# Causal keys cut in 128-blocks of one axis, and the order of the first stacks and shifts, in a four-layer attention kernel

## The chip, the cores and the metric

The kernel runs on one core of one Trainium2 chip. The metric is the device time of one launch in microseconds (us). TensorE is written PE in the rows, VectorE DVE, ScalarE ACT, GpSimd POOL, SyncE SP; SPq and ACTq are the queues on which SP and ACT issue DMAs.

## The reference

Four layers are applied to x (4 batches of 1024 tokens, 256 wide, 16 heads of 16). The change touches the first two; the third (attention with a given mask and weights) and the fourth (attention with folded weights) keep their code.

```
def _L0_xattn_ref(x, context, ...):
    qkv = (_ln(x, g1, be1) @ w_qkv + b_qkv).reshape(b, t, 3, h, dh)
    ckv = (context @ w_ckv + b_ckv).reshape(b, s, 2, h, dh)      # s = 77
    k = concatenate([k_self, k_ctx]); v = concatenate([v_self, v_ctx])
    scores = einsum('bthd,bshd->bhts', q, k) * scale
    mask = (j >= t) | (j <= i)           # own keys causal, context always seen
    x = x + softmax(where(mask, scores, -inf)) @ v
    x = x + gelu(_ln(_ln(x, g2, be2), gf, bf) @ w1 + b1) @ w2 + b2
def _L1_xattn_ref(x, encoder_out, ...):  # linear attention over the context and
    ...                                  # a causal window of 64 own keys, then Wout
    return residual + combined @ Wout
```

## The kernel before

The first three parts ("causal", the feed-forward "ff", and "window") are one program over one list of tokens, made by `front_order` (line 227). Every engine walks the same list and does its own part of each token, so the order of a token holds for all engines, SP's DMA issues included.

**The causal layer.** For each batch b, tokens are normalised (`stats`, `norm`, `flip`), projected to q and k (`qk`, `kc`), and cut into three bf16 terms (`high`, `middle`) that SP writes to DRAM (`zk`, `zq`). For each quad q of four heads SP reads them back as a stack (`stack`: 12 DMAs with the six products of terms on 96 rows, and for b = 0 one more, the row of ones from `zone`): `qs[q]` for the queries, `ks[q]` for the keys. Keys stand on one axis: 77 of the context first, then the 1024 own keys.

For a quad, the maximum of each query's scores is found first: `ring` tokens (56 a quad, lines 746 and 748 on TensorE, the maximum by VectorE at line 1016) pass through three PSUM banks (0, 1, 7). Then the `shift` token transposes the 32 x 128 maxima (L752), VectorE copies them to `nmT` (L1029), and ACT issues the DMA that puts them in row 96 of `qs[q]` (L847). The quad's first `scores` wait for that DMA (`shift_loaded`). The ring tokens of the next quad are spread over the first part of the main tokens of this quad by `spread`; the shift stands eight tokens before the quad's end, and no ring token stands behind it until the next quad starts.

The main work of a quad has two halves c of 512 queries, each made of steps (`causal_steps`, line 88). A step is one block of keys against n columns of queries: `scores` (L773: keys as the weights, four heads, two PSUM banks a shot, one or two shots), exp by ACT (L902), a diagonal mask by POOL where needed (L679), and `values` (L797: four heads side by side in the array, fp32), two steps later. Block 0 is the context (77 keys); the others are own keys by 128. So c = 0 has n = 512, 512, 384, 256, 128 and c = 1 has n = 512, 512, 384, 256, 128, 512, 512, 512, 512: 5632 columns and 24 shots a quad, over 16 quads. `vals` (L736) makes the values of each block; for the context it is two fp32 matmuls of 256 columns.

**Order around the change.** In the causal layer the list has stack 0 and stack 1 of batch 0, then `rest` (the loads of x of batches 1 to 3, L584), then the writes of the second half of the projections and the stacks 2 and 3; the ring of quad 0 follows. In the window layer, stack 0 of batch 0 waits for the last but one group of `down` products, and stack 1, 2 and 3 and the load of `wout` for the last `down`, since they lie in the memory of `hT`; `begin_rest` also has POOL's memset of v1 and VectorE's of the PSUM bank.

Of the kernel before, what the change touches and what calls it, by code (L numbers as in the profile page):

```python
# [33 lines left out]
P = 128  # L34
B, T, D, H, S = 4, 1024, 256, 16, 77
NT, ND = T // P, D // P
DH = D // H
# [49 lines left out]

def causal_steps(c):
# [66 lines left out]
def attention_tokens(ring_jobs, steps_of, nch, first):  # L155
# [76 lines left out]
def front_order():  # L232
# [18 lines left out]
    timed += [(0.6, (2, "begin")), (6.45, (2, "load_wc")), (7.99, stacks[0]), (10.0, (2, "begin_rest"))]  # L251
    timed += [(10.1, t) for t in stacks[1:]]
# [228 lines left out]
def attention_layer(nc, a, sem, x, ident, identb, masks, ctxT, banks, first, tiles_, zone, order, ring, before):  # L481
# [4 lines left out]
    steps_of = causal_steps if first else window_steps  # L486
    nch = 2 if first else 4
# [10 lines left out]
    if first:  # L498
        be, bcol, bcc, vrow, vcrow = (tiles_[n] for n in ("be", "bcol", "bcc", "vrow", "vcrow"))
# [4 lines left out]
    loaded, wc_loaded, wout_loaded, x_first, x_rest, wf_loaded, ones_saved = map(  # L504
        sem, ("loaded", "wc_loaded", "wout_loaded", "x_first", "x_rest", "wf_loaded", "ones_saved"))
    filled, const_ready, ones_ready, v_ready, cleared = map(sem, ("filled", "const_ready", "ones_ready", "v_ready", "cleared"))
    folded, tiled = sem("folded"), sem("tiled")
    nload = 8 + B if first else 3
# [37 lines left out]
    def sync(sp):  # L546
# [8 lines left out]
        def step(token):  # L555
            what, *args = token
            if what == "begin" and first:
# [6 lines left out]
                load_row(sp, vcrow, a["L0_xattn_b_ckv"][D:2 * D], loaded)  # L564
# [14 lines left out]
            elif what == "begin_rest":  # L579
                sp.wait_ge(*before["used"])  # L580
                load_weight(sp, wout, a["L1_xattn_Wout"], wout_loaded)
            elif what == "rest":
                for b in range(1, B):
                    sp.dma_start(x[:, b], a["x"][b].rearrange("(i p) d -> p i d", p=P)).then_inc(x_rest, 16)  # L584
# [5 lines left out]
            elif what == "stack":  # L590
# [27 lines left out]
    def gpsimd(pool):  # L618
# [28 lines left out]
        def step(token):  # L647
# [3 lines left out]
            if what == ("begin" if first else "begin_rest"):  # L651
# [4 lines left out]
                pool.memset(v1[:, :, :, DH:DH + 1], 1.0).then_inc(v_ready, 1)  # L656
            if what == "middle" or what == "high" and args[0]:
# [31 lines left out]
    def tensor(pe):  # L689
        started = set()  # L690
        def step(token):
# [38 lines left out]
            elif what == "vals":  # L730
                b, i = args
                rows = S if i < 0 else P
                for k in range(ND):
                    tokens_, wv = (ctxT[:, b, k, :], wc[:, k, D:2 * D]) if i < 0 else \
                        (xnT[:, k, i * P:(i + 1) * P], w[:, k, 2 * D:3 * D])
                    ins = pe.matmul(bk[0:rows, 0:D], tokens_, wv, start=k == 0, stop=k == ND - 1)  # L736
# [16 lines left out]
            elif what == "scores":  # L753
# [14 lines left out]
                for p_, pair in enumerate(pairs):  # L768
                    for side in range(2):
                        for blk, col, query, n in pieces:  # L770
                            key, nk = (0, S) if blk == 0 else (S + P * (blk - 1), P)
# [6 lines left out]
            elif what == "values":  # L778
# [15 lines left out]
                for blk, col, query, n, begins in one.gives:  # L794
                    rows = S if blk == 0 else P
# [30 lines left out]
    def scalar(act):  # L826
        def step(token):
# [57 lines left out]
            elif what == "scores":  # L885
# [7 lines left out]
                rows = S if pieces[0][0] == 0 else P  # L893
# [26 lines left out]
    def vector(dve):  # L920
        chain = Chain(dve, sem("chain"))
        def step(token):
# [23 lines left out]
            if token[0] == "stats" and token[1] == 1 and token[2] == 0 and first:  # L946
                dve.wait_ge(x_rest, 16 * (B - 1))
# [32 lines left out]
            elif what == "vals":  # L980
# [4 lines left out]
                rows = S if i < 0 else P  # L985
                dst = v1[0:rows, 1 + i, :, 0:DH]
                src = bk[0:rows, 0:D].rearrange("p (h d) -> p h d", d=DH)
                if first:
                    row = (vcrow if i < 0 else vrow)[0:rows, :].rearrange("p (h d) -> p h d", d=DH)
# [255 lines left out]
def front_layers(nc, a, sem, start, x, ident, identb, masks, ctxT, banks, masked):  # L1245
# [31 lines left out]
    def stacks(t, tag, put):  # L1277
        t["qs"], t["ks"] = [], []
        for q in range(NQ):
            t["qs"].append(put(f"qs{q}_{tag}", [KR + 1, QH, T], BF16))  # L1280
            t["ks"].append(put(f"ks{q}_{tag}", [KR + 1, QH, KW], BF16))
# [4 lines left out]
    stacks(causal, "causal", front)  # L1286
# [3 lines left out]
    for n, shape in (("wc", [P, ND, 2 * D]), ("xh", [P, NT // 2, D]), ("vrow", [P, D]), ("vcrow", [P, D]),  # L1290
                     ("be", [P, ND]), ("bcol", [P, 4]), ("bcc", [P, ND])):
# [17 lines left out]
    stacks(window, "window", Region(nc, start, LOW))  # L1309
# [3 lines left out]
    window["wc"] = top("wc_window", [P, ND, 2 * D])  # L1313
    window.update(common("window", top, middle, False))
# [3 lines left out]
    for n, shape in (("wout", [P, 4, D]), ("mixedT", [P, 2, 4, P])):  # L1318
        window[n] = top(f"{n}_window", shape)
# [11 lines left out]
              "half_used": (own_banks.ready, own_banks.filled(("down", 2 * B - 2, NT // 2 - 1))),  # L1331
# [939 lines left out]
```

## Time and profile before

| | us |
|---|---|
| runs | 2319.93, 2323.09, 2323.42 (median 2323.09) |
| the profiled execution | 2319.19 |
| its span | 2317.4 |
| mean granted clock of TensorE | 0.956 of full |

TensorE is busy 89% of the span, VectorE 61%, ACT 49%, POOL 31%. The causal layer lies at 0 to about 812 us, the feed-forward up to about 1049 us, the window layer from there to about 1600 us, and the two last layers behind it. In views of the timeline a row gives the start, the duration, the engine, the line, the operation and, in brackets, the idle time before it with what ended it; the end of a matmul is modelled and overlaps the next one, so its cost in a stream is read from the difference of two starts. An fp32 matmul leaves two records.

### The profile page before, as it was taken

Reading aid. Unit: us, or ns where it says so; the run is one execution under the profiler, and the core shown is the slowest. Engines: PE = TensorE matmul, PEld = TensorE weight load, DVE = VectorE, ACT = ScalarE, POOL = GpSimd, SP = SyncE. Lnnn points to the kernel's source line nnn. Section 1 sums busy time; section 2 is a strip of 40 time slices with the busy share of each in tenths; the row PEclk is TensorE's granted clock in tenths of the full one; section 3 lists DMA queues with packets and bytes.
Section 4 is the critical chain, followed back from the end, with each engine's and each line's share of the span. In section 5 each row is a group of like instructions: output and inputs, shape, how many; then the busy total and the mean of one; then the engine's idle time right before and its main releaser. Section 6 shows DMA issues by size and latency. Waiting matters only on the chain. (4 is left out here: it accounts for less than half of the span.)

```text
span 2317.4 us, 38184 instructions
## 1 busy us (share of the span) xinstructions
PE 2062.0 (89%) x14594; PEld 1348.2 (58%) x14594; DVE 1410.1 (61%) x3047; ACT 1132.6 (49%) x1675; POOL 729.1 (31%) x817
## 2 busy tenths in 40 slices
PE   4899999999998879996889898898989996999989
PEld 2333333343343268874466465665677775888989
DVE  4776686686768456644545455352577884766654
ACT  1265565555555666631444534444454554545444
POOL 2013113113212243411533616243301101555656
PEclk8799999999999999997999999999999998999999
DMA  5805402510630000018260613620422210000000
GB/s 122 154 6 91 76 1 60 90 23 32 111 73 1 1 14 1 10 56 125 57 115 9 135 29 67 105 65 18 141 96 83 83 56 1 8 13 12 15 12 20
DMA packets 77772, 126.65 MB, mean 55 GB/s; under 512 B 16652, under 2 KB 34828, under 8 KB 77584
## 3 DMA queue, kind: packets, MB, share of 16 engines
q1 hardware_dynamic: 74968, 122.63, 25.1%
q8 instruction: 118, 1.93, 0.4%
q10 hardware_dynamic: 2624, 1.58, 0.2%
q14 instruction: 62, 0.51, 0.1%
HBM read 93.59 MB, written 30.32 MB: 53 GB/s over the span
## 5 line engine op out<-in xcount | busy, mean ns | idle before, releaser
L1016 DVE TENSOR_REDUCE nmx_causal<-banks 128x1 f32<-128x333 f32 (+4 forms) x896 | 436.3, 537 | 174.0 <-PE banks L748 171.4
L902 ACT ACTIVATE probs_causal<-banks 128x1024 f32<-128x1024 f32 (+3 forms) x384 | 352.6, 952 | 281.0 <-PE banks L773 278.0
L748 PE MATMUL banks<-ks_causal,qs_causal 96*128 96x333 bf16 (+4 forms) x896 | 273.4, 342 | 11.9 <-DVE nmx_causal L1016 10.0
L679 POOL TENSOR_SCALAR_AFFINE_SELECT probs_window<-probs_window 128x512 f32<-128x512 f32 (+1 forms) x272 | 163.4, 608 | 307.1 <-ACT probs_window L902 296.7
L679 POOL TENSOR_SCALAR_AFFINE_SELECT probs_causal<-probs_causal 128x512 f32<-128x512 f32 x128 | 88.6, 693 | 510.6 <-ACT probs_causal L902 510.6
L773 PE MATMUL banks<-qs_causal,ks_causal 97*128 97x512 bf16 (+4 forms) x896 | 221.2, 344 | 23.6 <-DMA qs_causal<-nmT_causal 11.7
L1016 DVE TENSOR_REDUCE nmx_window<-banks 128x2 f32<-128x384 f32 (+2 forms) x320 | 140.7, 459 | 118.7 <-PE banks L748 116.8
L797 PE MATMUL banks<-probs_causal,v_causal 128*17 128x512 f32 (+4 forms) x1792 | 201.1, 522 | 0.0
L902 ACT ACTIVATE probs_window<-banks 128x768 f32<-128x768 f32 (+2 forms) x128 | 99.8, 783 | 129.2 <-PE banks L773 128.6
L748 PEld LDWEIGHTS banks<-ks_causal,qs_causal 96*128 96x128 bf16 x896 | 87.1, 100 | 112.7 <-DVE nmx_causal L1016 72.1
L746 PEld LDWEIGHTS banks<-below,identb 128*128 128x128 bf16 x512 | 50.2, 99 | 168.9 <-DVE nmx_causal L1016 115.3
L746 PE MATMUL banks<-below,identb 128*128 128x128 bf16 x512 | 117.7, 233 | 29.6 <-DMA ks_causal<-zk 17.3
L773 PEld LDWEIGHTS banks<-qs_causal,ks_causal 97*128 97x128 bf16 (+1 forms) x896 | 79.6, 103 | 109.0 <-ACT probs_causal L902 49.5
L2102 POOL TENSOR_TENSOR pT_folded<-full_folded,pT_folded 128x512 fp32r<-128x512 f32 (+1 forms) x96 | 104.6, 1107 | 96.3 <-ACT pT_folded L2199 96.3
L2141 PE MATMUL banks<-vw_folded,pT_folded 128*128 128x256 f32 x960 | 129.5, 287 | 0.0
L746 PE MATMUL banks<-near,identb 128*128 128x192 bf16 (+1 forms) x512 | 115.7, 260 | 15.1 <-DMA ks_window<-zk 7.6
L797 PE MATMUL banks<-probs_window,v_window 128*17 128x192 f32 (+3 forms) x1664 | 107.8, 338 | 21.8 <-ACT oT_window L913 18.9
L324 PE MATMUL banks<-fold_folded,xT_folded 128*128 128x308 f32 x768 | 120.4, 306 | 0.9 <-DVE pr_folded L2218 0.9
L2141 PEld LDWEIGHTS banks<-vw_folded,pT_folded 128*128 128x128 f32 x960 | 118.9, 190 | 0.0
L748 PE MATMUL banks<-ks_window,qs_window 96*128 96x192 bf16 (+1 forms) x512 | 115.0, 259 | 0.0
L773 PE MATMUL banks<-qs_window,ks_window 97*128 97x192 bf16 (+2 forms) x832 | 103.3, 251 | 12.4 <-DMA qs_window<-nmT_window 12.3
L324 PE MATMUL banks<-w_ff,hT 128*128 128x256 f32 x768 | 99.1, 287 | 14.2 <-DVE hT L1230 14.2
(251 smaller groups left out, 4105.0 us busy)
## 6 DMA issues: line engine op xcount, KB each, us to landing
fs_masked<-in_fside SPq DMA_DIRECT2D x32, 616.0 KB, 3.7
ks_causal<-zk SPq DMA_DIRECT2D x96, 137.6 KB
ks_window<-zk SPq DMA_DIRECT2D x96, 137.6 KB
qs_causal<-zq SPq DMA_DIRECT2D x96, 128.0 KB
qs_window<-zq SPq DMA_DIRECT2D x96, 128.0 KB
zk<-parts_causal SPq DMA_DIRECT2D x24, 275.2 KB, 2.5
zk<-parts_window SPq DMA_DIRECT2D x24, 275.2 KB, 2.6
zq<-parts_causal SPq DMA_DIRECT2D x24, 256.0 KB, 4.7
```

The costliest lines, as they stand in the source:

```text
L324: ins = pe.matmul(out, left, right, start=n == 0, stop=n == len(terms) - 1)
L679: pool.affine_select(out=v, in_=v, compare_op=ALU.is_ge, fill=0.0, base=const, pattern=[[0, QH], [by_c, wd]], channel_multiplier=by_p).the ...
L746: pe.matmul(bk[:, to:to + mn], identb[:], mask[:, m0:m0 + mn], start=True, stop=False, skip_group_check=True)
L748: ins = pe.matmul(bk[:, c:c + m], qs[q][0:KR, h, t * P:(t + 1) * P], ks[q][0:KR, h, key:key + m], start=cover is None, stop=True, skip_gro ...
L773: ins = pe.matmul(banks[0:nk, at + side, o:o + n], ks[q][0:kr, 2 * pair + side, key:key + nk], qs[q][0:kr, 2 * pair + side, q0:q0 + n], st ...
L797: ins = pe.matmul(banks[32 * h:32 * h + DH + 1, OUT, query:query + n], v1[0:rows, blk, QH * q + h, :], probs[0:rows, at % 3, h // 2, h % 2 ...
L902: ins = act.activation(dst, src, ACT.Exp, scale=DH ** -0.5)
L1016: dve.tensor_reduce(dst, src, AX.X, ALU.max, negate=True).then_inc(emptied_v, 1)
L2102: pool.tensor_tensor(dst[:, 1], full[:, full_of(token), 0:wd], dst[:, 0].bitcast(F32), ALU.subtract).then_inc(sem("lows"), 1)
L2141: ins = pe.matmul(out_of(b, i), pT[:, term[0], n % 2, c, :], vw[:, term[1], c, :], start=c == 0 and term == PARTS[0], stop=c == NPC - 1 an ...
```

## The change

Four things change.

(1) The keys of the causal layer are cut in blocks of 128 along the whole axis of 1101, context in front: block 0 has the 77 context keys and the first 51 own keys, block 8 the last 77 keys. A step then has n = 512, 461, 333, 205, 77 for c = 0 and 512, 512, 461, 333, 205, 77, 512, 512, 512 for c = 1: 5224 columns, again 14 steps and 24 shots a quad. Masks: 10 a quad in place of 8 (51, 128, 128, 128 and 77 columns wide), over as many columns in all. Block 0's values need both weight matrices: `vals` of block 0 becomes four matmuls, on a new zero-padded tile `pad` that POOL fills (one memset, and two copies a batch at the token `flip(b, 0, 1)`), with a bias row `vrow0` made of two DMAs.

(2) x of batch 1 is loaded at the start with its own semaphore; the loads of batches 2 and 3 (`rest`) move behind the stacks 2 and 3.

(3) For batch 0 of both layers, SP waits for the DMA of the first shift (`shift_loaded[0]`) before it issues the stacks 2 and 3.

(4) In the window layer `ks[1]` moves to the memory of the feed-forward's weights and `wout`, `mixedT` to that of `hT`; stack 1 waits for the last `up` instead of the last `down` and stands right behind stack 0, and `wout` is loaded behind the stacks 2 and 3.

```
+def causal_keys(blk):
+    return P * blk, min(P, KW - P * blk)
 def causal_steps(c):
-    ch, n0 = T // 2, T // 2 // P * c
-    blocks = [(0, 0)] + [(1 + n0 + m, m * P) for m in range(ch // P)] + [(1 + j, 0) for j in range(n0)]
+    first = T // 2 * c
+    starts = [P * blk - S - first for blk in range(-(-KW // P))]
+    seen = [blk for blk, at in enumerate(starts) if at < BANK]
+    late = [blk for blk in seen if blk and starts[blk] > -P]
     steps = []
-    for blk, c0 in blocks:
-        n = ch - c0
+    for blk in [0] + late + [blk for blk in seen if blk and blk not in late]:
+        c0 = max(0, starts[blk])
+        n = BANK - c0
...
-        masks = ((c0, P, 0, -1, 1),) if blk > n0 else ()
+        covered = min(BANK, starts[blk] + P) - c0
+        masks = ((c0, covered, c0 - starts[blk], -1, 1),) if covered > 0 else ()
...
-            if first and token[2] == 1:
-                order.append(("rest",))
+    order += [("rest",)] if first else []
...
-    timed += [(0.6, (2, "begin")), (6.45, (2, "load_wc")), (7.99, stacks[0]), (10.0, (2, "begin_rest"))]
-    timed += [(10.1, t) for t in stacks[1:]]
+    timed += [(0.6, (2, "begin")), (6.45, (2, "load_wc")), (7.99, stacks[0]), (8.0, stacks[1]), (10.0, (2, "begin_rest"))]
+    timed += [(10.1, t) for t in stacks[2:]] + [(10.2, (2, "load_wout"))]
...
+                sp.dma_start(x[:, 1], a["x"][1].rearrange("(i p) d -> p i d", p=P)).then_inc(x_second, 16)
...
-                        sp.wait_ge(*before["half_used" if q == 0 else "used"])
+                        for wait in before["stack"][min(q, 2)]:
+                            sp.wait_ge(*wait)
+                    if q >= 2:
+                        sp.wait_ge(shift_loaded[0], 16)
...
+            if what == "flip" and first and args[1:] == [0, ND - 1]:
+                b = args[0]
+                for k in range(ND):
+                    pool.wait_ge(*ring.emptied(("flip", b, 0, k)))
+                pool.tensor_copy(pad[:, 0, :, 0:S], ctxT[:, b]).then_inc(padded, 1)
+                pool.tensor_copy(pad[:, 1, :, S:P], xnT[:, :, 0:P - S]).then_inc(padded, 1)
...
+                elif i < 0:
+                    pe.wait_ge(padded, 1 + 2 * (b + 1))
+                    terms = [(pad[:, 0, k, :], wc[:, k, D:2 * D]) for k in range(ND)]
+                    terms += [(pad[:, 1, k, :], w[:, k, 2 * D:3 * D]) for k in range(ND)]
```

## Rows read from the trace of the kernel before

**Rows 1.** Timeline of the first shift, causal: start, us, engine.
```profile
81.80 0.60 ACTq L847 DMA_DIRECT2D qs_causal<-nmT_causal  x1
...
86.83 1.07 PE L773 MATMUL banks<-qs_causal,ks_causal 97*77 97x512 bf16 x2 [5.32 <-DMA qs_causal<-nmT_causal]
```

**Rows 2.** Timeline of the first shift, window layer.
```profile
1056.42 0.27 PE L746 MATMUL banks<-near,identb 128*128 128x128 bf16 x1 [7.61 <-DMA ks_window<-zk]
...
1065.56 5.59 SPq L606 DMA_DIRECT2D ks_window<-zk  x6
...
1067.38 0.53 ACTq L847 DMA_DIRECT2D qs_window<-nmT_window  x1
...
1079.41 1.44 PE L773 MATMUL banks<-qs_window,ks_window 97*128 97x192 bf16 x8 [12.31 <-DMA qs_window<-nmT_window]
```

**Rows 3.** All DMAs from nmT_window, by the view of that tile.
```profile
DMA to landing us min/median/max: 1.8/1.8/11.9
```

**Rows 4.** Stretches there: length, busy of PE, PEld, DVE, ACT, POOL; clock, DMA, GB/s.
```profile
1068.00:1072.00 4.00, 0.00 (x0) 0.00 (x0) 0.00 (x0) 1.22 (x1) 0.00 (x0) 0.55 1.11 146
...
1080.00:1085.00 5.00, 5.00 (x21) 3.57 (x19) 1.27 (x3) 1.51 (x2) 2.50 (x4) 0.50 1.07 139
```

**Rows 5.** What a causal score shot costs: two starts on PE.
```profile
254.01 0.60 PE L773 MATMUL banks<-qs_causal,ks_causal 97*128 97x512 bf16 x2
254.44 0.30 PE L748 MATMUL banks<-ks_causal,qs_causal 96*128 96x333 bf16 x1
```

**Rows 6.** PE from a shift to the next quad (quad 3 to batch 2).
```profile
268.40 0.22 PE L752 MATMUL banks<-identb,nmb_causal 128*32 128x128 bf16 x1 [0.28 <-DVE nmb_causal L1023]
...
269.08 0.41 PE L797 MATMUL banks<-probs_causal,v_causal 128*17 128x128 f32 x8
269.43 0.61 PE L773 MATMUL banks<-qs_causal,ks_causal 97*128 97x512 bf16 x2
270.55 0.60 PE L773 MATMUL banks<-qs_causal,ks_causal 97*128 97x512 bf16 x2 [0.51 <-ACT probs_causal L902]
271.08 1.05 PE L797 MATMUL banks<-probs_causal,v_causal 128*17 128x512 f32 x8
272.07 1.04 PE L773 MATMUL banks<-qs_causal,ks_causal 97*128 97x512 bf16 x4
273.04 1.05 PE L797 MATMUL banks<-probs_causal,v_causal 128*17 128x512 f32 x8
274.02 0.63 PE L773 MATMUL banks<-qs_causal,ks_causal 97*77 97x512 bf16 x2
```

**Rows 7.** Stretches of causal quads, columns as in rows 4.
```profile
258.00:266.00 8.00, 7.96 (x63) 3.41 (x62) 7.45 (x18) 2.81 (x4) 1.91 (x3) 1.00 0.01 2
266.00:274.00 8.00, 7.17 (x51) 1.60 (x48) 2.43 (x7) 6.73 (x8) 0.00 (x0) 1.00 0.01 1
...
274.00:299.00 25.00, 24.49 (x158) 13.22 (x155) 20.46 (x47) 8.25 (x10) 3.79 (x5) 1.00 0.51 66
299.00:322.00 23.00, 21.19 (x145) 7.00 (x146) 15.93 (x46) 16.72 (x19) 2.56 (x4) 0.93 0.01 1
322.00:338.00 16.00, 15.71 (x119) 6.50 (x111) 13.48 (x30) 9.58 (x12) 3.69 (x5) 1.00 0.01 1
...
486.00:508.00 22.00, 20.20 (x151) 7.07 (x148) 16.11 (x47) 16.94 (x20) 2.68 (x5) 1.00 0.01 2
```

**Rows 8.** PE's waits in the causal layer (60 to 830 us): us, times, longest.
```profile
PE banks L773 <- DMA qs_causal<-nmT_causal: 11.7, 4, 5.3
```

**Rows 9.** Groups: ACT's exp, and the context's values (108 to 810 us).
```profile
L902 ACT ACTIVATE probs_causal<-banks 128x1024 f32<-128x1024 f32 x224 | 220.0, 1024 | 135.6 <-PE banks L773 135.0
...
L736 PE MATMUL banks<-wc_causal,ctxT 128*77 128x256 f32 x12 | 3.1, 378 | 0.0
```

**Rows 10.** A tail in which the clock falls.
```profile
314.81 0.60 PE L773 MATMUL banks<-qs_causal,ks_causal 97*128 97x512 bf16 x2 [0.83 <-ACT probs_causal L902]
...
317.55 1.04 PE L773 MATMUL banks<-qs_causal,ks_causal 97*128 97x512 bf16 x2 [0.31 <-ACT probs_causal L902]
```

More of the change, by code:

```diff
@@ L486, in attention_layer @@
     steps_of = causal_steps if first else window_steps
+    keys_of = causal_keys if first else window_keys
     nch = 2 if first else 4
@@ L578, in step @@
                 load_weight(sp, wc, a["L1_xattn_Wkv"], wc_loaded)
-            elif what == "begin_rest":
-                sp.wait_ge(*before["used"])
+            elif what == "load_wout":
                 load_weight(sp, wout, a["L1_xattn_Wout"], wout_loaded)
             elif what == "rest":
-                for b in range(1, B):
+                for b in range(2, B):
                     sp.dma_start(x[:, b], a["x"][b].rearrange("(i p) d -> p i d", p=P)).then_inc(x_rest, 16)
@@ L656, in step @@
                 pool.memset(v1[:, :, :, DH:DH + 1], 1.0).then_inc(v_ready, 1)
+            if what == "begin" and first:
+                pool.memset(pad[:], 0.0).then_inc(padded, 1)
+                pool.wait_ge(padded, 1)
+            if what == "flip" and first and args[1:] == [0, ND - 1]:
[4 more added lines that the diff above has]
+                pool.tensor_copy(pad[:, 1, :, S:P], xnT[:, :, 0:P - S]).then_inc(padded, 1)
             if what == "middle" or what == "high" and args[0]:
@@ L731, in step @@
                 b, i = args
[L732 to L736, printed above, removed]
+                key, rows = keys_of(1 + i)
+                if not first:
+                    terms = [(ctxT[:, b, k, :], wc[:, k, D:2 * D]) if i < 0 else
+                             (xnT[:, k, i * P:(i + 1) * P], w[:, k, 2 * D:3 * D]) for k in range(ND)]
+                elif i < 0:
+                    pe.wait_ge(padded, 1 + 2 * (b + 1))
+                    terms = [(pad[:, 0, k, :], wc[:, k, D:2 * D]) for k in range(ND)]
+                    terms += [(pad[:, 1, k, :], w[:, k, 2 * D:3 * D]) for k in range(ND)]
+                else:
+                    terms = [(xnT[:, k, key - S:key - S + rows], w[:, k, 2 * D:3 * D]) for k in range(ND)]
+                for n, (tokens_, wv) in enumerate(terms):
+                    ins = pe.matmul(bk[0:rows, 0:D], tokens_, wv, start=n == 0, stop=n == len(terms) - 1)
             elif what == "ring":
@@ L794, in step @@
                 for blk, col, query, n, begins in one.gives:
-                    rows = S if blk == 0 else P
+                    rows = keys_of(blk)[1]
                     for h in range(QH):
@@ L892, in step @@
                 pairs, base, pieces = one.shots[k]
-                rows = S if pieces[0][0] == 0 else P
+                rows = keys_of(pieces[0][0])[1]
                 lo, hi = min(p_[1] for p_ in pieces), max(p_[1] + p_[3] for p_ in pieces)
@@ L984, in step @@
                     dve.wait_ge(probs_used, last_step(b - 1, NQ - 1, nch - 1) + 1)
-                rows = S if i < 0 else P
+                rows = keys_of(1 + i)[1]
                 dst = v1[0:rows, 1 + i, :, 0:DH]
@@ L988, in step @@
                 if first:
-                    row = (vcrow if i < 0 else vrow)[0:rows, :].rearrange("p (h d) -> p h d", d=DH)
+                    row = (vrow0 if i < 0 else vrow)[0:rows, :].rearrange("p (h d) -> p h d", d=DH)
                     ins = dve.tensor_tensor(dst, src, row, ALU.add)
@@ L1280, in stacks @@
             t["qs"].append(put(f"qs{q}_{tag}", [KR + 1, QH, T], BF16))
-            t["ks"].append(put(f"ks{q}_{tag}", [KR + 1, QH, KW], BF16))
+            t["ks"].append((put_second if q == 1 else put)(f"ks{q}_{tag}", [KR + 1, QH, KW], BF16))
     front = Region(nc, start, MID)
     causal = {}
-    stacks(causal, "causal", front)
+    stacks(causal, "causal", front, front)
     top = Region(nc, start + MID, ARENA - MID)
@@ L1313, in front_layers @@
     window["wc"] = top("wc_window", [P, ND, 2 * D])
+    low = Region(nc, start, LOW)
+    stacks(window, "window", low, top)
     window.update(common("window", top, middle, False))
```

36 lines of the change are left out of this document (21 added, 15 removed).

## The prediction

> **What bounds the kernel now.** I read the page first: TensorE is busy 89% of the span, so a change that takes columns from TensorE looks as if it paid in full. Then I cut the causal layer into stretches and laid the starts of TensorE's instructions beside what they must cost. The cost in a stream is seen in the starts: a score shot half of two 512-column bf16 matmuls takes 254.44 - 254.01 = 0.43 us [rows 5], 0.42 ns a column and head; a values step of four heads takes 272.07 - 271.08 = 0.99 us at 512 columns and 269.43 - 269.08 = 0.35 us at 128 [rows 6], so 1.67 ns a column for the four together. Added up over whole quads this accounts for 74 to 86% of the time only. The reader is to see in the stretches what takes the rest. In quad 3, away from its end, VectorE is busy 7.45 of 8.00 us from 258 to 266 us [rows 7]: there the ring (56 maxima a quad, through three banks) sets the pace, and TensorE's "7.96" is a modelled end that hides its waits. In the first halves of quads 0 and 1 VectorE has 20.46 of 25 and 13.48 of 16 us, and TensorE is the fuller one: both share the bound. In the tail of a quad, from the shift to the next quad, VectorE is nearly idle (2.43 of 8.00 us), ACT has 6.73, and the second of two shots waits 0.51 us for the exp of the one before the last [rows 6]: the tail is a chain of shot, exp, shot.
>
> Two stalls stand apart. TensorE waits 5.32 us for the first shift's DMA in the causal layer [rows 1], and 12.31 us in the window layer [rows 2], while the 16 DMA engines are full with the stacks (1.11, 146 GB/s [rows 4]).
>
> **The first shift, causal.** ACT issues it at 81.80 and TensorE starts at 86.83, 5.0 us later [rows 1]. SP issues stack 2 from 80.2 on, just ahead of it. After the change those stacks wait for the shift, and nothing else is in flight at 82 us: stack 1 ends about 66, and the six writes of the projections' second half come right behind it, since the x loads no longer stand in between. The median DMA from nmT lands in 1.8 us [rows 3], so TensorE starts about 1.9 us after the issue: **-3.1 us**. Behind SP's new wait stand stack 2, stack 3 and the x loads of batches 2 and 3. A stack is 1.64 MB, 11.7 us at 140 GB/s; two of them and 2 MB of x end near 120 us. Stack 2 is first read by the ring in quad 1's stretch at 134 us, x of batch 2 past 270 us. So the wait costs nothing. x of batch 1 (1 MB) is issued at about 10 us in a stretch in which SP has nothing to issue until 27 us, and is wanted at 104 us: 0, at worst 1 us if it slows the bias rows.
>
> **The first shift, window.** Ring 0 starts at 1056.42, when stack 0 has landed, and ACT issues the shift at 1067.38 [rows 2]. Stack 1 now follows stack 0 at once, so it ends near 1056.4 + 11.7 = 1068.1; the shift meets only its end. I take 2.3 us to TensorE's start instead of 12.0: **-9.7 us**. Bounds: -12.0 (no latency at all) and -7 (it lands like the causal one, 5.0 us, beside other loads). The stacks 2 and 3 and wout then end near 1069.7 + 23.4 + 3.7 = 1097 us; quad 1's stretch, which reads stack 2, starts at 1105 us, less 10 is 1095, with stack 2 in by 1082; stack 3 and wout are wanted later, and the next writes of SP come at 1124 us. No cover is lost. TensorE runs at 1.2 GHz after the long stall (0.50 from 1080 to 1085 [rows 4]) and the clock had already fallen at 1068 to 1072 (0.55). So the shorter stall probably doesn't keep it; I take 0, within -3 to +1.
>
> The Trainium skill (DMA: Bandwidth & Descriptors, section "Queues, rings and completion order") says that an engine takes the queues in turn, packet by packet. By that alone ACT's small DMA would hardly be late behind SP's stacks; the 11.9 us of rows 3 says that it is, so I go by the row.
>
> **The blocks.** A quad loses 5632 - 5224 = 408 columns. On TensorE that is 408 x 4 x 0.42 ns = 0.68 us of scores and 408 x 1.67 ns = 0.68 us of values, 1.36 us a quad and 21.8 us over 16 quads, if all of it were on the path. ACT loses 408 x 4 elements of exp, at 1024 ns for 1024 elements [rows 9] at most 1.6 us a quad, off the path but in the tail. VectorE loses nothing: the ring is as it was. Against it, block 0's values take two more fp32 matmuls a batch, 3.1 us / 3 = 1.03 us each batch at most (12 records are three batches) [rows 9]: 4.1 us, and 3.5 us by TensorE's starts. Where in the quad do the columns go? 204 in c = 0 (four steps, 51 each), 0.68 us, less some 0.08 for a 77-column shot, in which the four weight loads don't shrink: 0.6 us. In c = 1 three steps grow by 77 and one full step of 512 becomes one of 77, which is a net -0.1 us under the ring and -0.6 us in the tail (values of 128 become 205, those of 512 become 77: 0.48 + 0.27 for 0.35 + 0.99).
>
> In quad 3's tail that -0.6 us doesn't shorten the chain of exps: the shot at 270.55 still waits for its exp; the shots at 272.07 go one by one as the exps end at about 271.5 and 272.5, so the last values start at about 272.95 instead of 273.04: -0.1 us. Quad 2's tail is held by the shift's DMA (the other three waits of the 11.7 us, 6.4 us [rows 1, 8]), 0. Quad 1's tail is full of projections, so there it counts: -0.6 us. For the 0.6 us of c = 0 I take 0.4 in quad 0, 0.3 in quad 1, 0.35 in quad 2 (by VectorE's share in rows 7: where it is at 82% two thirds count, at 84% half, at 93% a quarter) and 0.15 in quad 3. A batch: 1.2 + 0.8 = 2.0 us, four batches 8 us, and 1 us more for the very last quad, which has no ring behind it and goes at ACT's pace: **-9 us**, and **+3.5** for block 0's values. Bounds: nothing of it counts (+4.1 us in all), or all (-21.8 + 3.5 = -18.3 us).
>
> The 32 added masks and eight copies are POOL's, which sits idle before nearly every mask; a values step comes two steps behind its mask. 0. The copies wait for both flips of a half; behind them stand masks of steps that ACT has not done yet. 0, at most 0.3 us a batch.
>
> **The clock.** TensorE does less in tails of the same length, and there the clock is near its fall. In the tail of quad 0 of batch 1, with waits of 0.83 and 0.31 us, the matmul pair at 317.55 takes 1.04 us instead of 0.60 [rows 10]; that stretch has a clock of 0.93 where its twin of batch 2 has 1.00 (299 to 322 and 486 to 508 us) [rows 7]. The two halves last 23.7 and 22.2 us, from one context step to the next (298.8 to 322.6 and 486.1 to 508.2 us): 1.5 us for one fall. I expect two more such falls, **+2.5 us**.
>
> **Sum** against the profiled execution: 2319.19 - 3.1 - 9.7 - 9 + 3.5 + 2.5 = 2303.4 us. That execution lies 3.9 us below the median of the runs, so the median after is 2307.3; I say 2307.
>
> **Rivals.** First: the columns pay in full. For it: TensorE's 89%, and its 15.71 of 16 us in the first half of quad 1. Against it: VectorE's 7.45 of 8. Then -12.8 - 18.3 = -31.1: 2292. Second, on the other side: the clock falls in the tails. The values step of 77 columns takes 0.27 us where there was 0.99 us of work, so waits of about 0.2 and 0.5 us come before the two shots of 272.07, right behind the one of 0.51 [rows 6]; the fall of rows 10 came after waits of 0.83 and 0.31 us, also close together. At 1.5 us a fall, all 15 tails give +22.5 on a sum without the 2.5: 2323.09 - 18.3 + 22.5 = 2327. It outweighs all gains from 12 falls on and is slower beyond doubt from 15; falls of 2 us under the ring bring that to 11. For it: rows 10; against it: the tail of rows 6, with 0.51 us of waiting, keeps the full clock.
>
> The Trainium skill names this pattern (TensorE: Matmul & The Clock Gate, section "A second HAM failure mode: psum-queue depth-cycling"): small idle times between groups of matmuls make the clock swing between its two levels. The trace agrees once in this place (0.93 in rows 7), not in its twin.
>
> Third: the order doesn't do what it says in the window layer. The shift still meets stack 1, or ACT's DMA is slow for another reason, and lands after 7 us: -5 instead of -9.7: 2312. For it: stack 1's end and the shift's issue are 1 us apart.
>
> **Chances.** Forecast 0.58 (2300 to 2314), first rival 0.14, second 0.15 (0.08 of it slower, 0.07 within the bound), third 0.08, the rest 0.05 within the bound. 0.2%, 4.6 us, is what a measurement of this kernel can tell. Faster 0.80, same 0.12, slower 0.08. The range from 2293 to 2317 takes in the first rival's near end and up to six falls.
>
> **What would show it.** The waits of TensorE for the DMA from nmT at about 84 and 1070 us: gone or about 2 us each; the first quad's scores at 83.7. VectorE's share under the ring of quad 3 stays at or above 93%, and the distance from one shift to the next there shrinks by less than 0.5 us, while quad 1's second half shrinks by about 0.7. The clock of the stretches that are tails: 1.00 except in two or three. If the halves of quad 3 shrink by 0.6 us each, the bound was TensorE after all and the first rival holds; if the mean clock falls below 0.95, the second. I am wrong also if a wait for `padded` or a mask shows on TensorE, or if ring 1 of the window layer waits for its stack.

## The result and the profile after

The changed kernel takes 2309.61 us (median of 6 runs, 2299.41 to 2313.20), the kernel before, on the same chip, 2323.26 us (median of 6, 2317.73 to 2335.86). The ratio is 0.9937, with a 95% interval of 0.9915 to 0.9959: 14 us faster, 9 to 20. Forecast were 2307 us and 16 us faster. Three executions in which the chip was disturbed (3273 us of the repeat below, 2609 and 10741 us of the order alone) are left out of all numbers, and the two profiles among them are not read. The profiled execution of after took 2313.20 us (span 2311.5), which makes it the slowest of the six; it is only 6 us shorter than the profiled one of before, and part of what follows is to find the other 8 us.

The first part of the page of the kernel after, and from its part on groups the three that the blocks shorten:

```profile
PE 2053.5 (89%) x14610; PEld 1348.9 (58%) x14610; DVE 1409.0 (61%) x3047; ACT 1112.0 (48%) x1675; POOL 739.2 (32%) x858
...
L940 ACT ACTIVATE probs_causal<-banks 128x1024 f32<-128x1024 f32 (+5 forms) x384 | 331.0, 898 | 292.3 <-PE banks L811 288.7
...
L811 PE MATMUL banks<-qs_causal,ks_causal 97*128 97x512 bf16 (+5 forms) x896 | 211.5, 332 | 27.5 <-ACT probs_causal L940 14.7
...
L835 PE MATMUL banks<-probs_causal,v_causal 128*17 128x512 f32 (+5 forms) x1792 | 187.0, 490 | 0.0
```

The work went as the diff says: the causal exps are busy 331.0 us where they were 352.6, the scores 211.5 for 221.2, the values 187.0 for 201.1. TensorE alone sheds 24 us there. The time shed is 14 us, and most of that comes from elsewhere.

The first shift of the causal layer, in the timeline of after (start, duration, engine; in brackets the wait before it):

```profile
80.08 0.60 ACTq L885 DMA_DIRECT2D qs_causal<-nmT_causal  x1
...
81.99 1.03 PE L811 MATMUL banks<-qs_causal,ks_causal 97*128 97x512 bf16 x2 [2.19 <-DMA qs_causal<-nmT_causal]
82.31 1.73 SPq L626 DMA_DIRECT2D qs_causal<-zq  x4
```

From ACT's issue to TensorE's first scores are 1.91 us, where [rows 1] have 5.03: -3.1 us. SP's stack of quad 2 now comes after it (82.31). The same place of the window layer:

```profile
1043.00 2.77 SPq L626 DMA_DIRECT2D ks_window<-zk  x6
1048.98 0.26 PE L784 MATMUL banks<-near,identb 128*128 128x128 bf16 x1 [9.27 <-DMA ks_window<-zk]
...
1060.21 0.53 ACTq L885 DMA_DIRECT2D qs_window<-nmT_window  x1
...
1062.13 1.44 PE L811 MATMUL banks<-qs_window,ks_window 97*128 97x192 bf16 x8 [2.20 <-DMA qs_window<-nmT_window]
```

1.92 us for 12.03 in [rows 2]: -10.1 us. A little may be given back at once. Stack 1 follows stack 0 without a gap, and stack 0 lands 16.1 us after its first issue (1032.87, the issue of its zone, to 1048.98), where it took 14.5 before (1041.96 to 1056.42): +1.7 us here. In the seven other profiles with this order it takes 14.6 to 16.0 us, 15.2 in the mean, so about 0.7 of the 1.7 us comes with the order and the rest is scatter. The stretches of after at the restart of that layer, and one under the ring of quad 3 (length, then busy time of PE, PEld, DVE, ACT, POOL, the granted clock, DMA share, GB/s):

```profile
1060.00:1062.00 2.00, 0.00 (x0) 0.00 (x0) 0.18 (x1) 1.23 (x1) 0.00 (x0) 1.00 0.02 4
1062.00:1067.00 5.00, 4.87 (x27) 3.83 (x27) 1.34 (x4) 1.56 (x3) 2.49 (x4) 0.66 0.74 117
1067.00:1072.00 5.00, 5.00 (x30) 4.19 (x29) 3.39 (x9) 0.00 (x0) 0.00 (x0) 1.00 1.08 136
253.00:261.00 8.00, 7.52 (x65) 3.25 (x64) 7.18 (x17) 2.74 (x4) 1.94 (x4) 1.00 0.01 2
```

After the short stall the clock falls for a few us (0.66) and is whole again from 1067 us; after the long one it was at 0.50 from 1080 to 1085 us, in full work [rows 4]. From the first window scores to the second shift are 23.6 us instead of 24.9. But this too is mostly chance: the seven other profiles with the short stall have 24.3 to 24.8 us, and in the repeat below the clock is at 0.50 from 1069 to 1074 us, right behind a stall just as short. So the shorter stall gives 0 to 0.6 us, as forecast. Under the ring of quad 3 VectorE still has 7.18 of 8 us (7.46 from 251 to 259 us).

Where the 6 us between the two profiled executions come from can be read from the starts of the copies to `nmT` (one a shift, 16 a layer). The start is 1.7 us earlier, which no edit explains; the first distance of the causal layer is 3.4 us shorter, its other fourteen 2.0 us together; the distance behind the window layer's first shift gives 11.4 us, and 2.1 of this sum of 18.6 are lost in the batch that follows (quad 2 and the first boundary). There after leads by 16.5 us. Then it loses 9.2 us in two places, the boundaries to the third and fourth batch, and 1.5 us behind the layer. The first of the two, in after:

```profile
1299.42 0.51 ACTq L885 DMA_DIRECT2D qs_window<-nmT_window  x1
1304.41 2.67 SPq L626 DMA_DIRECT2D qs_window<-zq  x6
1304.78 0.82 PE L811 MATMUL banks<-qs_window,ks_window 97*128 97x192 bf16 x4 [1.92 <-DMA qs_window<-nmT_window]
```

The shift lands 5.3 us after its issue, behind earlier stacks, TensorE waits 1.92 us for it, and from 1306 to 1312 us its clock is 0.50. At the next boundary it is 2.60 us and 0.50 again. In a second profile of the same kernel (below) no matmul waits at either place and the distances are 47.3 and 46.7 us instead of 50.7 and 53.1. So these 9.2 us are not in every execution of the changed kernel; whether the change makes such late shifts more frequent, these profiles can't tell. With them taken out the two profiles are 15 us apart, close to the 14 of the medians.

### The profile page after: what moved, and what is told of

Its sections match the earlier page's. It is cut to its first block and busy times, and to the rows that moved or that the text cites. A ratio compares the mean times of both kernels' runs of the same rounds, so it can differ in the third digit from the quotient of the medians.

```text
span 2311.5 us, 38268 instructions
## 1 busy us (share of the span) xinstructions
PE 2053.5 (89%) x14610; PEld 1348.9 (58%) x14610; DVE 1409.0 (61%) x3047; ACT 1112.0 (48%) x1675; POOL 739.2 (32%) x858
## 5 line engine op out<-in xcount | busy, mean ns | idle before, releaser
L940 ACT ACTIVATE probs_causal<-banks 128x1024 f32<-128x1024 f32 (+5 forms) x384 | 331.0, 898 | 292.3 <-PE banks L811 288.7
L709 POOL TENSOR_SCALAR_AFFINE_SELECT probs_causal<-probs_causal 128x512 f32<-128x512 f32 (+2 forms) x160 | 97.8, 612 | 514.4 <-ACT probs_causal L940 514.1
L811 PE MATMUL banks<-qs_causal,ks_causal 97*128 97x512 bf16 (+5 forms) x896 | 211.5, 332 | 27.5 <-ACT probs_causal L940 14.7
L835 PE MATMUL banks<-probs_causal,v_causal 128*17 128x512 f32 (+5 forms) x1792 | 187.0, 490 | 0.0
```

The lines of the kernel that those rows point to most:

```text
L709: pool.affine_select(out=v, in_=v, compare_op=ALU.is_ge, fill=0.0, base=const, pattern=[[0, QH], [by_c, wd]], channel_multiplier=by_p).the ...
L811: ins = pe.matmul(banks[0:nk, at + side, o:o + n], ks[q][0:kr, 2 * pair + side, key:key + nk], qs[q][0:kr, 2 * pair + side, q0:q0 + n], st ...
L835: ins = pe.matmul(banks[32 * h:32 * h + DH + 1, OUT, query:query + n], v1[0:rows, blk, QH * q + h, :], probs[0:rows, at % 3, h // 2, h % 2 ...
L940: ins = act.activation(dst, src, ACT.Exp, scale=DH ** -0.5)
```

## The experiments

Each ratio is to the kernel before on the same chip.

**The changed kernel again**, to know what two executions of the same program differ by. No edit.

> The changed kernel once more, unchanged, for a second profile. In the first profile of it the shifts of quad 3 in batches 1 and 2 of the window layer landed late behind stack loads, TensorE waited 1.9 and 2.6 us and its clock fell, which gave back 3.4 and 5.8 us of 16.5 us won by then; before, both landed in time. My theory: that is chance of the DMA's timing, which this profile has at other places or sizes (each boundary between quads 2 and 3 of the causal and the window layer 0 to 6 us off), with the time 12 to 16 us below the kernel before. Rival: it belongs to the change; then the same two boundaries are late again by 3 to 6 us. Stays in either case: first shifts in about 1.9 us, quad 3's ring part at 33.3 us.

Measured: 2305.18 us (median of 11), ratio 0.9939 [0.9919, 0.9960]. A repeat with one more profile:

> The changed kernel once more for a profile at full clock, since that of e1 fell in a disturbed run. Theory that the late shifts of quad 3 in batches 1 and 2 of the window layer are chance: each of the six distances from the shift of quad 2 or 3 around them differs from the first profile by up to 6 us. Rival (they belong to the change): the distances from shift to shift there are again 50.7 and 53.1 us, within 0.5.

Measured: 2316.16 us in one run, span 2314.4. The two distances that were 50.7 and 53.1 us are 47.3 and 46.7, so the rival is out. The two profiles of this kernel differ, for one, in the tail of quad 0 of batch 1. First the profile after (clock third from the end), then its timeline from the same tail:

```profile
309.00:315.00 6.00, 5.13 (x37) 1.27 (x38) 0.86 (x3) 5.03 (x6) 0.00 (x0) 1.00 0.01 1
315.00:321.00 6.00, 6.00 (x44) 2.44 (x42) 5.20 (x11) 3.87 (x5) 0.87 (x2) 1.00 0.01 3
```

```profile
311.27 0.60 PE L811 MATMUL banks<-qs_causal,ks_causal 97*128 97x512 bf16 x2 [0.37 <-ACT probs_causal L940]
...
313.11 0.61 PE L811 MATMUL banks<-qs_causal,ks_causal 97*128 97x512 bf16 x2 [0.31 <-ACT probs_causal L940]
313.64 1.05 PE L835 MATMUL banks<-probs_causal,v_causal 128*17 128x512 f32 x8
```

The same in the repeat:

```profile
312.00:318.00 6.00, 5.63 (x35) 1.10 (x34) 0.86 (x3) 4.73 (x6) 0.00 (x0) 0.68 0.01 1
318.00:324.00 6.00, 6.00 (x36) 2.17 (x29) 2.93 (x7) 2.91 (x4) 0.39 (x1) 0.75 0.01 3
```

```profile
314.02 0.91 PE L811 MATMUL banks<-qs_causal,ks_causal 97*128 97x512 bf16 x2 [0.37 <-ACT probs_causal L940]
...
315.26 1.89 PE L811 MATMUL banks<-qs_causal,ks_causal 97*128 97x512 bf16 x4
317.07 1.91 PE L835 MATMUL banks<-probs_causal,v_causal 128*17 128x512 f32 x8
```

The waits are the same to 0.01 us; in one execution the clock stays, in the other it falls to its lower level (1.2 GHz), and the values of 512 columns take 1.91 us for 1.05. The distance from shift to shift is 47.84 instead of 45.30 us there: 2.5 us a fall. The repeat has two of them, in the tails of quad 0 of batches 1 and 2. (Its distance in batch 3 is long too, 47.85 us for 46.27, but there the clock is whole in the tail and low from 710 to 725 us, in the quad's work.) The same two tails keep 45.28 to 45.30 us in the profile after and in four other profiles with these blocks (the blocks alone, and three kernels with a hold below): two falls in twelve tails. With the old blocks it is one in four, in the profile before (47.30 us for 45.75). The second rival needed twelve falls.

**The blocks alone**, the order of the kernel before:

```diff
-                    if q >= 2:
-                        sp.wait_ge(shift_loaded[0], 16)
...
-    timed += [..., (7.99, stacks[0]), (8.0, stacks[1]), (10.0, (2, "begin_rest"))]
-    timed += [(10.1, t) for t in stacks[2:]] + [(10.2, (2, "load_wout"))]
+    timed += [..., (7.99, stacks[0]), (10.0, (2, "begin_rest"))]
+    timed += [(10.05, (2, "load_wout"))] + [(10.1, t) for t in stacks[1:]]
... (all loads of x back behind stack 1, stack 1 of the window layer back behind the last `down`)
```

> The changed kernel with the old order of SP's work: the x loads behind stack 1, no wait for the first shift, stack 1 of the window layer and wout behind the last down. Only the keys in 128-blocks are left. My theory (VectorE's ring and the exps of the tail hold the quads): 2 to 6 us faster than the kernel before, ring part of quad 3 unchanged at 33.3 us, tail 5.6 to 5.5 us; TensorE waits 5 us and 12 us for the first shifts, as before. Rival (TensorE's columns pay in full): 18 us faster.

Measured: 2319.36 us, ratio 0.9991 [0.9972, 1.0010]. TensorE waits 5.5 and 11.5 us for the two first shifts, about as before.

**The order alone**, the steps and values of the kernel before:

```diff
-    for blk in [0] + late + [blk for blk in seen if blk and blk not in late]:
+    blocks = [(0, 0)] + [(1 + n0 + m, m * P) for m in range(ch // P)] + [(1 + j, 0) for j in range(n0)]
... (and keys_of = window_keys, no pad, the two-matmul values of the context)
```

> The changed kernel with the old steps of the causal layer (context as block 0, own keys by 128), the two-matmul values of the context and no padded tile; only the order of the loads, shifts and stacks is changed. My theory: 12 to 14 us faster than the kernel before (3.1 in the causal, 9.7 in the window layer). Rival (the shift's DMA is slow for another reason than SP's stacks, or another load gets late): under 6 us.

Measured: 2309.23 us (median of 10), ratio 0.9953 [0.9930, 0.9977]. So the order is worth 11 us (5 to 16) of the 14, the blocks 2 us with an interval that includes none. TensorE sheds 24 us of busy time by the blocks and the program gets 2. Its waits for the shift's DMA in the causal layer (us, times, longest) have grown. First in the kernel with the blocks alone, then in the kernel after:

```profile
PE banks L809 <- DMA qs_causal<-nmT_causal: 14.4, 4, 5.5
```

```profile
PE banks L811 <- DMA qs_causal<-nmT_causal: 12.1, 4, 3.9
```

[rows 8] have 11.7 in four waits, 5.3 of it in the first and 6.4 in the three others, one in each tail of quad 2 of batches 0 to 2. In the kernel after the first is 2.2, and the three others have grown to 9.9; with the blocks alone they are 8.9. It looks as if TensorE waited there for what it saves ahead of that wait. The starts say otherwise. SP issues the first of the next batch's stacks 19.26 us ahead of the copy to `nmT` in all three places of the kernel after, and 20.64, 20.64 and 19.19 us ahead of it before: in the first two the profile before has a fall of the clock (0.65 from 219 to 223 us, and 407 to 411) that delayed the shift but not the stacks. The shift lands 27.0 to 28.4 us after that first issue in all six places, so a later shift waits less: that is 2.9 of the 3.5 us. From the copy to where TensorE begins to wait are 5.32 us for 5.43, so the blocks put 0.1 us into each wait, and the rest is scatter: in four profiles with the same blocks and no hold in this layer single waits of these go from 1.6 to 4.1 us. The clock falls behind these waits before (0.57 to 0.66) as it does after. The kernel after there:

```profile
208.64 3.30 SPq L626 DMA_DIRECT2D ks_causal<-zk  x6
...
211.98 0.42 SPq L566 DMA_DIRECT2D zq<-parts_causal  x1
212.45 0.91 SPq L566 DMA_DIRECT2D zk<-parts_causal  x2
213.40 0.90 SPq L566 DMA_DIRECT2D zq<-parts_causal  x2
...
219.82 0.51 ACTq L885 DMA_DIRECT2D qs_causal<-nmT_causal  x1
...
228.77 0.60 PE L811 MATMUL banks<-qs_causal,ks_causal 97*128 97x512 bf16 x2 [3.89 <-DMA qs_causal<-nmT_causal]
```

SP has issued the next batch's stacks 0 and 1 (200.31 to 211.94 us, 3.3 MB) and behind them five writes of projections (to 214.3 us, 1.3 MB). The writes land about 16 us after their issue, at 228 to 230 us, and the shift of quad 3, 8 KB, lands with them, 8.9 us after its own. So it comes in when nearly all that SP had issued ahead of it is done. That gives the next experiment.

**Stack 1 held behind the shift of quad 3**, in both layers, for batches 1 to 3:

```diff
                 if b:
                     sp.wait_ge(scores_ready, last_shot(b - 1, q))
+                    if q == 1:
+                        sp.wait_ge(shift_loaded[1], 16 * (shift_number[b - 1, NQ - 1] // 2 + 1))
```

> The changed kernel with one more wait of SP: for batches 1 to 3 of both layers the stack of quad 1 is issued only when the shift of quad 3 of the batch before has landed. My theory: the shifts of quad 3 land late because they meet the loads of that stack and the writes behind it. Then they land in about 2 us, the wait of TensorE for the DMA from nmT goes to under 1 us at these six places, the distance from the shift of quad 3 to the next quad's first scores falls from 8 to 9.4 us to 5.5 us in the causal layer (3 x 3 us), the clock doesn't fall there (2 us each), and the kernel is 10 to 20 us faster than the changed one, 24 to 34 us than before. Rival: what is in flight there is the stack of quad 0 or the writes already issued; then under 3 us from the changed kernel. Second rival, on the other side: the stack of quad 1 or 2 comes late for its ring, and the time is 0 to 10 us longer than the changed kernel's.

Measured: 2289.26 us, ratio 0.9848 [0.9818, 0.9879]: 30 us below the median of the kernel before on the same chip (2319.78), 35 by the ratio. Against the changed kernel it is 16 us by the medians and 21 by the ratios. The timeline of this kernel:

```profile
201.87 2.66 SPq L628 DMA_DIRECT2D qs_causal<-zq  x6
...
221.37 0.51 ACTq L887 DMA_DIRECT2D qs_causal<-nmT_causal  x1
...
223.29 2.65 SPq L628 DMA_DIRECT2D qs_causal<-zq  x6
...
226.36 0.60 PE L813 MATMUL banks<-qs_causal,ks_causal 97*128 97x512 bf16 x2
```

and its waits of PE for that DMA in the causal layer:

```profile
PE banks L813 <- DMA qs_causal<-nmT_causal: 2.2, 1, 2.2
```

Only the first shift is waited for. SP issues in order, so the hold keeps the writes behind stack 1 (now at 228.79 us) behind the shift too; which of the two delayed it was not tried apart. From the shift of quad 3 to the next are 37.2 us three times, where the kernel after has 42.8, 41.5 and 43.6 (40.8 to 41.4 before): 5.4 us each, of which 3.3 are the wait. The rest, 2.1 us, fits the clock: it falls in all three of these tails in the kernel after (0.78 from 227 to 231 us, 0.57 and 0.61 in the two others) and in none with the hold. In each layer alone:

```diff
-                    if q == 1:
+                    if q == 1 and first:            # the other kernel: and not first
```

> The changed kernel with the held stack of quad 1 in the causal layer alone. My theory (the shifts of quad 3 land late behind that stack): nearly all of the gain of e4 is here, since in two profiles of the changed kernel the distance from the shift of quad 3 to the next was 41.5 to 43.6 us three times and 37.2 us in e4: 14 to 17 us faster than the changed kernel. Rival (the gain of e4 is shared by both layers, the window's late shifts being frequent): 6 to 10 us.

Measured: 2290.12 us, ratio 0.9867 [0.9843, 0.9891].

> The changed kernel with the held stack of quad 1 in the window layer alone. My theory: 0 to 4 us faster than the changed kernel, since the late shifts there are chance (9.2 us lost in one profile, nothing in the other), and less scattered. Rival, as in e9: 8 to 12 us faster.

Measured: 2306.46 us, ratio 0.9924 [0.9894, 0.9953]. Against the ratio of the changed kernel (0.9937) these are -16 and -3 us, and -21 for both. The causal layer has nearly all of it; 3 us for the window layer are within what such medians tell.

**The hold with the old blocks** asks what the blocks are worth once no late shift hides their gain:

```diff
+                    if q == 1:
+                        sp.wait_ge(shift_loaded[1], 16 * (shift_number[b - 1, NQ - 1] // 2 + 1))
... (causal steps, keys and values of the kernel before)
```

> The held version (e4) with the old steps of the causal layer (context as block 0, own keys by 128, two-matmul values). Its distance to e4 is what the blocks are worth once the late shifts are gone. My theory (VectorE's maxima set the pace under the ring, exps in the tail): 2 to 5 us slower than e4, with the distance from shift to shift the same within 0.2 us where quad 3's ring runs, 0.5 to 1.5 us longer in quads 1 and 2. Rival (the blocks' gain was hidden by the late shifts): 10 to 18 us slower than e4.

Measured: 2292.74 us, ratio 0.9868 [0.9849, 0.9886]. The median with the new blocks is 3.5 us lower and the ratio 0.0020 (4.6 us), each within the intervals. Between the two profiles the sixteen causal shifts end 3.4 us earlier with the new blocks (674.0 for 677.5 us from first to last). Each of the two middle batches gains 0.27 us in the distance from the shift of quad 3 on, 0.46 in quad 1's, 0.07 in quad 2's, and quad 0's is 0.08 longer with block 0's values in it. In the first and the last batch quad 1's distance gains 1.15 and 1.31 us (the last with falls of the clock in both profiles), and quad 0's is 0.42 and 0.11 longer; quad 2's is the same within 0.07 in the first and 0.28 longer in the last. I had expected 0.5 to 1.5 us in quad 2's.

I had put most of it into the tail of quad 1, since projections fill it. That tail with the old blocks:

```profile
352.51 0.60 PE L809 MATMUL banks<-qs_causal,ks_causal 97*128 97x512 bf16 x2
...
355.11 1.04 PE L809 MATMUL banks<-qs_causal,ks_causal 97*128 97x512 bf16 x4
356.08 1.05 PE L833 MATMUL banks<-probs_causal,v_causal 128*17 128x512 f32 x8
...
359.27 0.63 PE L809 MATMUL banks<-qs_causal,ks_causal 97*77 97x512 bf16 x2
```

and with the new ones (the kernel of the hold):

```profile
350.55 0.60 PE L813 MATMUL banks<-qs_causal,ks_causal 97*128 97x512 bf16 x2
...
354.25 0.33 PE L837 MATMUL banks<-probs_causal,v_causal 77*17 77x77 f32 x8
355.00 0.60 PE L813 MATMUL banks<-qs_causal,ks_causal 97*128 97x512 bf16 x2 [0.43 <-ACT probs_causal L942]
355.92 0.61 PE L813 MATMUL banks<-qs_causal,ks_causal 97*128 97x512 bf16 x2 [0.31 <-ACT probs_causal L942]
...
357.44 0.60 PE L813 MATMUL banks<-qs_causal,ks_causal 97*128 97x512 bf16 x2
```

From the first row to the next quad's first scores are 6.76 us with the old blocks and 6.89 with the new. The 0.72 us that the values step of 77 columns sheds (0.33 for 1.05) have become two waits for ACT's exp, 0.43 and 0.31 us, which the old tail didn't have; the 205 columns that the step ahead of it now has cost their time as well. This tail too is a chain of shot, exp, shot, with a projection in it.

**Maxima over fewer columns**, to take VectorE's share away (the maxima of the causal ring then cover the first 128 columns of each bank only, so the shift is not the reference's). On the old blocks with the hold and on the new ones with the hold:

```diff
                 src = bk[:, 0:t * n].rearrange("p (t n) -> p t n", t=t)
+                if first:
+                    src = src[:, :, 0:P]
```

> As e5, but in the causal layer VectorE takes the maximum over the first 128 columns only of each ring piece (the shift is then a maximum over fewer keys). This takes about 10 us a quad from VectorE, so the ring no longer sets the pace. Base for the next run; I expect it 30 to 90 us faster than e5.

Measured: 2247.93 us, ratio 0.9667 [0.9649, 0.9686].

> As e4 (new blocks, held stack), with the same short maxima as e6: the maximum over the first 128 columns only of each ring piece. My theory: with VectorE out of the way TensorE's columns come nearer to paying, so it is 9 to 16 us faster than e6 (18.3 us in full, less the tails that exps hold), against 2 to 5 us between e5 and e4. Rival (the columns don't pay because something else, ACT's exps or the waits between engines, holds every quad): the distance to e6 stays within 2 to 5 us.

Measured: 2246.73 us, ratio 0.9666 [0.9644, 0.9689]. If VectorE were all that hides the columns, the two would lie 9 us or more apart. The medians say 1 us, and by the two intervals this is uncertain by an estimated 7 us either way, so 16 us are out and 9 barely. The spans of the two profiles are 9.1 us apart, but the one with the new blocks is the fastest execution of its four; over the sixteen causal shifts they differ by 6.6 us (636.8 for 643.4), and 4.3 us of that are two falls of the clock in the third batch of the old blocks. Without them a middle batch gains 1.0 us, where it gained 0.7 with VectorE loaded. Quad 3's ring with VectorE unloaded, in the kernel with the new blocks:

```profile
226.00:234.00 8.00, 7.82 (x66) 3.76 (x63) 5.01 (x20) 5.55 (x7) 1.09 (x3) 1.00 1.06 161
```

VectorE is down to 5.01 us of 8, from 7.66 in the same place with all columns (242.7 to 250.7 us of the kernel with the hold), and there the blocks are worth 0.71 us a quad instead of 0.27. In quad 0, block 0's values included, they are worth 0.93 us instead of -0.08. Quad 2's distance, on the contrary, is 1.2 us longer with the new blocks (50.5 for 49.3). The timeline and the stretches of that kernel at its end:

```profile
369.34 0.23 PE L786 MATMUL banks<-below,identb 128*128 128x128 bf16 x1 [1.70 <-DVE mixed_causal L1095]
```

```profile
367.00:371.00 4.00, 2.30 (x19) 1.08 (x19) 3.50 (x9) 1.45 (x2) 4.00 (x3) 0.89 0.77 99
371.00:375.00 4.00, 4.00 (x26) 1.12 (x18) 1.30 (x5) 0.86 (x1) 0.94 (x3) 0.68 0.01 4
```

and the same place with the old blocks:

```profile
368.00:372.00 4.00, 2.45 (x21) 1.53 (x25) 3.79 (x10) 1.02 (x1) 4.00 (x3) 1.00 1.10 131
```

TensorE waits 1.70 us there for VectorE's sum of the outputs (1.55 with the old blocks), and the clock falls, at this place in all three batches, with the old blocks in one of three. So a part of what the blocks save is paid back in clock in this profile. Whether the longer wait causes the falls was not tried, and three against one are few.

## Why the prediction came out right, and where its steps did not

**The first shifts.** Forecast -3.1 and -9.7, measured -3.1 and -10.1 us from issue to scores; the order alone took 11 us off. What stack 1 costs stack 0 I had left out: +1.7 us in this profile, about 0.7 over all. For the clock at the restart I had taken 0 within -3 to +1; -1.3 in this profile, 0 to -0.6 in the others. The third rival, the shift still late behind stack 1, is out: TensorE starts 1.9 us after the issue. Nothing behind SP's new wait was missed: the other DMAs that TensorE waits for, in the whole kernel, are the two stacks 0, of the causal and of the window layer.

**The columns.** Forecast -9 + 3.5 = -5.5 us; measured -2 by the ratio with the order of before, -3.5 to -4.6 with the hold, and -3.4 in its profiles from the first causal shift to the last, where -4.5 was summed. The first rival (-18.3) is out. By terms, for a middle batch: quad 3's 0.15 came as 0.27; VectorE's pace holds it (7.18 to 7.46 of 8 us, 90 to 93%, where the sign asked for 93), and its tail is 0.1 us shorter, 5.50 for 5.62 [rows 6], as forecast. Quad 0's 0.5, less 0.87 for block 0's values, should have made it 0.4 longer, and it is 0.08 longer (0.42 in the first batch); quad 1's 0.3, and 0.1 of the tail before it, came as 0.46, and as over 1 us in the first and last batch. The term that fails is quad 1's tail: "Quad 1's tail is full of projections, so there it counts: -0.6 us". It comes to nothing; the time became two waits for exps, the same two that I had foreseen at 0.2 and 0.5 us for quad 3's tail. With it quad 2's distance gains 0.07 us where 0.95 were summed (0.35 of it for its own first half). So the -3.4 lies near the -4.5 in part by luck: quad 1 and quad 0 gave more than their terms, quad 2 gave nothing. Why quad 1 gains more in the first batch than in the middle ones stays open.

**Quad 2's tail** I had put at 0, "held by the shift's DMA". That holds: the blocks bring TensorE to the wait 0.1 us earlier, and the end of the wait doesn't move with it. The three waits grew from 6.4 to 9.9 us in the profile after, but 2.9 us of this are two falls of the clock that the profile before had ahead of them. What I missed is their size as a place to gain: I priced them at 6.4 us and left them, and the hold took 16 us from them in the causal layer alone.

**The copies and block 0's values.** The values of block 0, by group over 108 to 810 us of the kernel after:

```profile
L774 PE MATMUL banks<-wc_causal,pad_causal 128*128 128x256 f32 x12 | 3.1, 378 | 0.0
L774 PE MATMUL banks<-w_causal,pad_causal 128*128 128x256 f32 x12 | 3.1, 379 | 0.0
```

The second row is the added work: 3.1 us in three batches, 1.03 us each, as forecast, and no wait for the padding or a mask stands on TensorE.

**The clock.** Forecast were two falls more, at 1.5 us each; the sum has them as +2.5 where its own price makes 3.0. No term of this size shows. In the tails of quad 0 the falls are two in twelve with the new blocks and one in four with the old; ahead of the end of quad 2 the profile before has two, 1.45 us each, and six profiles with the new blocks have none; in the tails of quad 2 the clock falls behind the waits before as after, and with the hold in neither. The mean clock of after is 0.955 for 0.956. So the number is chance from execution to execution, and a fall can cost 1 us more than I took; two of them are 5 of the 17 us between the fastest and the slowest run of this kernel. The second rival would need twelve falls and is out, its mechanism is not: the Trainium skill (TensorE: Matmul & The Clock Gate, section "A second HAM failure mode: psum-queue depth-cycling") says that small idle times between groups of matmuls make the clock swing. The repeat has such a fall right behind waits of 0.37 and 0.31 us, while the other profile keeps 1.00 after the very same waits.

The forecast stood within 3 us of the median because most of the gain came from two stalls, whose 13 us were read right to within 2, and partly by luck: the blocks gave 1 to 3.5 us less than the 5.5 forecast, and the +2.5 for the clock, which no run shows, stood against that.

## What to carry to other kernels

Look at what a small transfer shares the DMA engines with when it is issued, at every place where it recurs and not only where its wait is longest: two first shifts gave 11 us, the three later ones of the same kind, 2 us of wait each in the profile before, another 16. Columns taken from the busiest engine pay only where no chain or second engine sets the pace; in the tails of this kernel, chains of shot, exp, shot, they turned into waits. And when a wait grows from one profile to another, look first whether the clock fell ahead of it in one of them. The larger lever here is VectorE: maxima over 128 columns, though the kernel then leaves out most of each maximum, took 42 to 45 us off. The version to keep is the change with stack 1 held behind the shift of quad 3: 2289 us, 30 us below the kernel before and 16 below the changed one on the same chip, by the medians.

## What the runs showed of the hardware

A DMA of 8 KB from ACT's queue lands in 1.8 us when nothing else is in flight, and in 5 to 12 us behind SP's stacks and writes (5.3 at 1299 us, 8.9 at 219 us, 11.9 in [rows 3]). All DMAs from `nmT_causal`, first in the kernel after, then with the hold:

```profile
DMA to landing us min/median/max: 1.8/1.8/8.9
```

```profile
DMA to landing us min/median/max: 1.8/1.8/2.8
```

The Trainium skill (DMA: Bandwidth & Descriptors, section "Queues, rings and completion order") has the engines take the queues in turn, by packets. By that alone the hold would have gained next to nothing; it gained 16 us, and the shift at 219.82 us landed together with the writes that SP had issued by 214.3, so here the bytes already issued on the other queue do delay a late small DMA. Which part of the path makes it wait was not measured.

The clock falls or stays after waits equal to 0.01 us. No single profile can tell whether a change makes falls more frequent; over the tails of quad 0 of one kernel it was none in one profile and two in the other.
